# Twelve weight transfers issued from inside the first attention, and two attentions that normalise their own input

## The reference

```python
# layer 0, attention (retention-like decay on the probabilities)
q, k, v = split(layernorm(x) @ W_attn)         # 128 -> 3 x 128, 16 heads of 8
probs   = softmax(q k^T / sqrt(8), masked) * decay
x       = x + (probs v) @ W_proj

# layer 1, attention (no projections: the normed input itself is scaled)
xn    = layernorm(x)                            # eps 1e-5, no gain
q, k  = xn * rotation, xn * entangle
x     = x + softmax(q k^T / sqrt(8)) xn
```

## Time and profile before

| | |
|---|---|
| median of three executions | 1744.04 us |
| the profiled execution's own time | 1747.32 us |
| its span in the trace | 1745.5 us |
| mean granted TensorE clock | 0.922 |
| TensorE matmul busy | 1506.1 us (86%) |
| VectorE busy | 1171.3 us (67%) |
| ScalarE busy | 902.2 us (52%) |
| GpSimd busy | 716.9 us (41%) |
| layernorm block of the first attention begins | 12.14 us |
| first row maximum of the first attention | 30.34 us |
| layernorm block of layer 1's attention begins | 347.6 us |
| first row maximum of layer 1's attention | 358.17 us |

### The profile page before, as it was taken

How to read it: one execution, slowest core, us unless ns; L and a number is a source line. 1 busy time by engine, 2 the same in 40 slices (tenths; PEclk the granted TensorE clock), 3 DMA queues, 4 the chain that set the end, 5 groups by cost and what they waited for, 6 DMA issues and landing times. The chain is left out here.

```text
span 1745.5 us, 28828 instructions
## 1 busy us (share of the span) xinstructions
PE 1506.1 (86%) x9987; PEld 965.2 (55%) x9987; DVE 1171.3 (67%) x2471; ACT 902.2 (52%) x2612; POOL 716.9 (41%) x674
## 2 busy tenths in 40 slices
PE   4998767879889999978899879999958877679998
PEld 2565535545567765443334337888744343357776
DVE  4887573469777765537998887777767785544443
ACT  2775332257677762226776646777724342444443
POOL 2557251122564441217888882333522234431000
PEclk8999986989999999978999999999979786889999
DMA  6000000000000000020000000000000000000000
GB/s 283 1 2 1 2 2 1 0 1 1 2 2 2 2 1 1 2 87 1 0 1 1 0 1 2 2 2 2 2 0 1 0 1 1 1 1 7 7 6 7
DMA packets 3165, 18.95 MB, mean 11 GB/s; under 512 B 592, under 2 KB 720, under 8 KB 2256
## 3 DMA queue, kind: packets, MB, share of 16 engines
q1 hardware_dynamic: 3024, 17.14, 2.4%
HBM read 16.09 MB, written 1.05 MB: 10 GB/s over the span
## 5 line engine op out<-in xcount | busy, mean ns | idle before, releaser
L827 POOL TENSOR_TENSOR l_xattn_probs<-l_xattn_probs,l_xattn_recip 128x512 f32<-128x512 f32 x128 | 133.3, 1042 | 222.8 <-DVE l_xattn_recip L766 222.4
L999 ACT ACTIVATE l_attn_probs<-ps,l_attn_neg_max 128x128 f32<-128x128 f32 x512 | 145.1, 384 | 74.0 <-DVE l_attn_neg_max L1048 72.2
L2547 POOL TENSOR_TENSOR l_mamba_hc<-l_mamba_h,l_mamba_c 128x512 f32<-128x512 f32 x128 | 159.2, 1272 | 0.0
L2449 DVE TENSOR_TENSOR_SCAN l_mamba_h<-ps,l_mamba_dBx 128x512 f32<-128x512 f32 x128 | 152.6, 1211 | 1.8 <-ACT ps L2346 0.7
L2219 PE MATMUL ps<-l_mamba_hc,w_const 128*128 128x512 f32 x256 | 136.6, 637 | 19.5 <-POOL l_mamba_hc L2547 16.5
L3195 DVE SCALAR_TENSOR_TENSOR xn<-ps,l_gates,xn 128x128 f32<-128x128 f32 x224 | 63.2, 344 | 121.7 <-PE ps L2852 120.8
L761 DVE COPY l_xattn_probsT<-ps 128x512 f32<-128x512 f32 x128 | 87.9, 687 | 71.3 <-PE ps L613 71.3
L2985 ACT ACTIVATE wkv<-ps,w_early 128x512 f32<-128x512 f32 x112 | 70.8, 684 | 115.5 <-PE ps L2841 115.4
L2852 PEld LDWEIGHTS ps<-w_early,wkv 128*128 128x128 f32 x896 | 109.1, 194 | 28.6 <-issue 18.7
L2852 PE MATMUL ps<-w_early,wkv 128*128 128x128 f32 x896 | 111.3, 278 | 8.8 <-ACT wkv L2985 8.8
L712 ACT ACTIVATE l_xattn_probs<-ps,l_xattn_neg_max 128x128 f32<-128x128 f32 x256 | 91.9, 389 | 41.3 <-DVE l_xattn_neg_max L756 41.3
(11 more groups left out here) (523 smaller groups left out, 3666.1 us busy)
## 6 DMA issues: line engine op xcount, KB each, us to landing
w_early<-in_l_moe SPq DMA_DIRECT2D x1, 3669.0 KB, 12.1
w_l_xattn<-in_l_xattn SPq DMA_DIRECT2D x1, 2176.0 KB, 22.6
w_early<-in_l_xattn SPq DMA_DIRECT2D x1, 1890.0 KB, 15.4
w_l_attn<-in_l_attn SPq DMA_DIRECT2D x1, 1242.0 KB, 24.6
ctx<-in_ctx SPq DMA_DIRECT2D x1, 1088.0 KB, 11.1
x<-in_x SPq DMA_DIRECT2D x2, 512.0 KB, 4.4
ctxT<-in_ctxT SPq DMA_DIRECT2D x1, 1024.0 KB, 9.0
out_x<-x SPq DMA_DIRECT2D x4, 256.0 KB, 2.8
```

The costliest lines, as they stand in the source:

```text
L827: nc.gpsimd.tensor_tensor(probs[:, D % 2, n, :, :], probs[:, D % 2, n, :, :], along(recip[:, D % 2, n, :], [P, HALF, P]), ALU.mult).then_i ...
L999: ins = nc.scalar.activation(probs[:, t % 4, g, :], S_of(t)[:, g * P:(g + 1) * P], ACT.Exp, bias=neg_max[:, t % 2, g:g + 1], accum_out=total)
L2449: nc.vector.tensor_tensor_scan(flat(h[:, t % 2, half, :, :]), G.ps[:, DA_BANK[half], :], flat(dBx[:, t % 2, half, :, :]), 0.0, ALU.mult, A ...
L2547: nc.gpsimd.tensor_tensor(heads4(hc[:, t % 4, half, :]), h[:, t % 2, half, :, :], c_sb[:, t % 3, :, :], ALU.mult).then_inc((hc0_set, hc1_s ...
```

## The change

The first block issues four transfers only: blocks 0 to 7 of `x`, the constants, blocks 8 to 15 of `x`, the first attention's weights. The other twelve are issued by SyncE at the start of the attention's own block (`load_rest`). In the first block VectorE takes the statistics of all 16 blocks and the variances of the first eight, and GpSimd their scales. Both narrow attentions lose their layernorm block: they build a `Lead` with banks 4, 5, 6 and 6, and its pieces are woven into their own lists. Quads 0 and 1 are transposed ahead of step 0, quad 2 in step 0 and quad 3 in step 1, each behind the scores. For the first attention GpSimd makes the last scales and normals before the first keys, for layer 1's after them. The small constants move to the start of VectorE's list, the `q_scale` of layer 1 too.

```diff
-def narrow_attention(nc, G, tag, w=None, q_scale=None):
+def narrow_attention(nc, G, tag, w=None, q_scale=None, prepare=None):
...
+        O_BANK, X_BANK = 6, 7
+        lead = Lead(nc, G, s, tag, (4, 5, O_BANK, O_BANK))
...
+        @block.sync
+        def _(sp):
+            if first:
+                load_rest(nc, G, sp)
+            lead.sync(sp)
...
             def project(b):
+                lead.wait(pe, b)
...
+            pe.wait_ge(G.loaded["const"], 16)
+            lead.needs(pe)
+            lead.tensor(pe, 0)
             if projected:
                 project(0)
+                pe.wait_ge(consts, 1)
                 pe.wait_ge(p_taken, 1)
-            else:
-                pe.wait_ge(masked, 2)
+            lead.tensor(pe, 1)
             for t in range(STEPS + OUT_LAG + 1):
                 b, s_ = at(t)
                 if t < STEPS:
                     scores(t)
                 if projected and s_ == 0 and b + 1 < NB:
                     project(b + 1)
+                if t < 2:
+                    lead.tensor(pe, 2 + t)
                 if T_LAG <= t < STEPS + T_LAG:
+                    if t == T_LAG:
+                        lead.wait(pe, QUAD)
                     turn(t - T_LAG)
                 if V_LAG <= t < STEPS + V_LAG:
+                    if t == V_LAG:
+                        lead.wait(pe, NB - 1)
                     times_v(t - V_LAG)
...
+            lead.scalar(act, 0)
             if projected:
                 act.wait_ge(masked, 2)
                 take(0)
+            lead.scalar(act, 1)
             for t in range(STEPS + V_LAG + 1):
...
                 if projected and s_ == 0 and b + 1 < NB:
                     take(b + 1)
+                if t < 2:
+                    lead.scalar(act, 2 + t)
...
+            lead.rest.early(dve, nc.vector, 0, 0)
+            dve.wait_ge(G.loaded["const"], 16)
+            if first:
+                small_constants(nc, G, dve).then_inc(consts, 1)
+            if prepare:
+                lead.needs(dve)
+                prepare(dve)
             heads = G.c["heads"].rearrange("p (r i) -> p i r", r=4)
             nc.vector.tensor_reduce(mask4[:], heads, AX.X, ALU.max).then_inc(masked, 1)
             nc.vector.memset(v_sb[:, :, :, DH:VP], 0.0).then_inc(masked, 1)
...
+            lead.rest.variances(dve)
+            for q in range(1, lead.rest.first // QUAD):
+                lead.rest.early(dve, nc.vector, 0, q)
+            lead.rest.late(dve, nc.vector, 0)
             for t in range(STEPS + OUT_LAG + 1):
...
+            lead.rest.early(pool, nc.gpsimd, 1)
             pool.wait_ge(masked, 2 if projected else 3)
-            keys(0)
+            if projected:
+                lead.rest.scales(pool)
+                lead.rest.late(pool, nc.gpsimd, 1)
+                keys(0)
+            else:
+                keys(0)
+                lead.rest.scales(pool)
+                lead.rest.late(pool, nc.gpsimd, 1)
...
 def l0_attn(nc, G):
-    layernorm(nc, G, "l0_attn", "l0_attn")
     narrow_attention(nc, G, "l0_attn", w=G.w["l0_attn"])
...
-        layernorm(nc, G, "l1_attn", "l1_attn", also=prepare)
-        narrow_attention(nc, G, "l1_attn", q_scale=q_scale[:])
+            dve.wait_ge(own, 1)
+
+        narrow_attention(nc, G, "l1_attn", q_scale=q_scale[:], prepare=prepare)
...
+    @G.first.vector
+    def _(dve):
+        for b in range(NB):
+            if b % (NB // 2) == 0:
+                dve.wait_ge(G.loaded[f"x{b // (NB // 2)}"], 16)
+            if b == begun.first:
+                begun.variances(dve)
+            begun.stats(b)
+        dve.wait_ge(begun.seen, NB)
+
+    @G.first.gpsimd
+    def _(pool):
+        nc.gpsimd.memset(G.neg_half[:], -0.5).then_inc(exponent, 1)
+        pool.wait_ge(exponent, 1)
+        begun.scales(pool)
+
+
+def load_rest(nc, G, sp):
+
+    for group in LAYOUT:
+        if group == "l0_mlstm":
+            sp.dma_start(G.ctxT[:], G.aps["ctxT"]).then_inc(G.loaded["ctxT"], 16)
+            sp.dma_start(G.ctx1, G.aps["ctx1"]).then_inc(G.loaded["ctx1"], 16)
+        if group not in ("const", "l0_attn", "l3_moe"):
+            sp.dma_start(G.pack[group], G.aps[group]).then_inc(G.loaded[group], 16)
```

More of the change, by code:

```diff
@@ L851, in narrow_attention @@
     OUT_LAG = V_LAG + (2 if projected else 1)
+    first, G.started = not G.started, True
     with Scope(nc, G, tag) as s:
@@ L866, in narrow_attention @@
         (masked, p_made, p_taken, q_set, v_set, k_ready, scored, maxed, exped, row_summed, row_inverted, evened, turned, copied, summed,
-         o_copied, o_turned, inverted, normed, out_made, added) = (s.sem(n) for n in (
+         o_copied, o_turned, inverted, normed, out_made, added, consts) = (s.sem(n) for n in (
              "masked", "p_made", "p_taken", "q_set", "v_set", "k_ready", "scored", "maxed", "exped", "row_summed", "row_inverted",
-             "evened", "turned", "copied", "summed", "o_copied", "o_turned", "inverted", "normed", "out_made", "added"))
+             "evened", "turned", "copied", "summed", "o_copied", "o_turned", "inverted", "normed", "out_made", "added",
+             "consts"))
+        O_BANK, X_BANK = 6, 7
+        lead = Lead(nc, G, s, tag, (4, 5, O_BANK, O_BANK))
         ahead = Ahead(nc, G, s, twice=not projected)
         DONE = OUT_LAG + U * ahead.first
-        O_BANK, X_BANK = 6, 7
         Q, K, V, E = (slice(n * P, (n + 1) * P) for n in range(4))
@@ L1074, in keys @@
                 else:
+                    lead.wait(pool, b)
                     source = G.xnT[:, b, :]
@@ L3388, in _, with load @@
             received_normals(LAST)
-def load(nc, G, aps):
+def load(nc, G, aps, with_stats):
+    s = Scope(nc, G, "load")
+    begun = Ahead(nc, G, s, first=NB // 2) if with_stats else None
+    exponent = s.sem("exponent")
     @G.first.sync
@@ L3401, in _ @@
               .then_inc(G.loaded[f"x{n}"], 16)
-        for group in LAYOUT:
-            if group == "l3_moe":
-                continue
+            group = ("const", "l0_attn")[n]
             sp.dma_start(G.pack[group], aps[group]).then_inc(G.loaded[group], 16)
-            if group == "l0_attn":
-                sp.dma_start(G.ctxT[:], aps["ctxT"]).then_inc(G.loaded["ctxT"], 16)
-                sp.dma_start(G.ctx1, aps["ctx1"]).then_inc(G.loaded["ctx1"], 16)
+    if not with_stats:
+        return
+    @G.first.vector
[19 more added lines that the diff above has]
+            sp.dma_start(G.pack[group], G.aps[group]).then_inc(G.loaded[group], 16)
 def small_constants(nc, G, dve):
@@ L3416, in small_constants @@
     nc.vector.tensor_copy(G.rows3_bf[:], G.c["rows3"])
-    nc.vector.tensor_copy(G.mask_qk_bf[:], G.c["mask_qk"])
     nc.vector.tensor_copy(G.mask_kq_bf[:], G.c["mask_kq"])
+    return nc.vector.tensor_copy(G.mask_qk_bf[:], G.c["mask_qk"])
 def store(nc, G, out):
@@ L3487, in program @@
             G.first = first
-            load(nc, G, aps)
+            load(nc, G, aps, (sublayers or SUBLAYERS)[0] is l0_attn)
         for sublayer in sublayers or SUBLAYERS:
```

## The result

The changed kernel takes 1735.89 us in the median (1721.68 to 1740.54, 20 executions), the kernel before 1744.53 (1734.31 to 1755.77, 20). The medians differ by 8.6 us, or 0.5%. The ratio of the means is 0.9934 (11.5 us), 95% interval 0.991 to 0.9959: faster, clear of noise and by under 1%. The forecast was 1735.1 us. The profiled execution has a span of 1736.6 us against 1745.5, 8.9 less, which is the very sum that was forecast. That it fits to the decimal is luck: two of the parts came out better than forecast, one worse, and that is what the rest of this is about.

A forecast was written before the change was run, and what follows sets the result against it. Serial links from each narrow attention's start to its first row maximum were taken as the bound. 6.0 us in the first attention plus 2.9 in layer 1 gave 8.9, from 1744.04 to 1735.1 us; the forecast's own range 1727 to 1743.

The forecast's parts named there:

- The first block: Start: second half of `x` lands at 8.0 us, the attention's block opens at 11.1 instead of 12.18.
- Rival (d): Start: moved issues don't free it, as `x`'s second half lands late; at 12 us, 4 us go: 1739; chance 0.05.
- The first preamble: First attention up to its first row maximum: keys done at 20.15, row maximum at 23.3, 7.0 us earlier.
- Given back in steps 0 and 1: First attention: transposes of quads 2 and 3 between the scores cost 1.0 us, between 0.5 and 2.0, leaving 6.0 gained.
- rival (b): First attention and layer 1: TensorE's clock stays up, both ramps save 2 to 3 us more each; 1730; chance 0.08.
- Layer 1: Layer 1's attention: first row maximum 4.4 us earlier, 1.5 us given back before the third scores, 2.9 us gained.
- rival (c): TensorE's clock stays at half into the full steps because it waits twice; four such steps lose 15 us: 1750; chance 0.07.
- The port: VectorE and GpSimd normals: exclusion would delay first keys by up to 1.6 us, first attention giving 4.4; left out of the sum.
- The stages between take the time they took: Stages between first attention and layer 1's attention: sign that their time stays unchanged, 0 us gained.
- everything later follows at its own pace: Opening claim: only the stretches up to each attention's first row maximum matter; what follows keeps its pace.
- The sum: Whole kernel: 6.0 from the first attention plus 2.9 from layer 1, 8.9 us gained.

The follow-up runs named there:

- the mLSTM experiment: The kernel before plus one wait keeping GpSimd's last two pairs of query quads until VectorE's five row operations are done; 1742.78 us, ratio 0.9958.

## Why the prediction was right, point by point

- **The first block** held. `x` landed at 4.79 and 7.85 us (said: 4.5 and 8.0), the block opened at 11.04 (11.1), and the late issue was worth 1.07 us by the experiment that took it back (1.1). Rival (d) is out.
- **The first preamble** held: keys done at 20.17 (20.15), first row maximum at 23.32 (23.3). The sum of row durations carried the whole serial chain to 0.1 us.
- **Given back in steps 0 and 1** failed. I took 1.0 us; the piece gained 8.0 and not 6.0. 7.0 of the 8.0 lie ahead of the first row maximum, as forecast, so from there to the stage's end the new form took 0.95 us less, not 1.0 more. The second row maximum came 4.86 us after the first, before 3.49, but only a part of that is quad 2: where the old code's second scores ran at half pace too, in the mLSTM experiment, it was 4.45. And the third scores took 1.13 us after and 2.02 before, and the ramp was faster from there. That looks like rival (b), for this stage alone; I had priced it at 2 to 3 us and given it 0.08. It is not the change's own doing as far as the runs show. From first row maximum to end the old code took 141.95, 141.95 and 140.93 us in three kernels, the new code 140.6 to 142.2 in the seven without idle matmuls there besides the changed kernel's 141.00. The two ranges overlap: neither a loss of 1.0 us nor a gain can be told from how the clock happened to run, and the 1.0 us was a term too much.
- **Layer 1** held in its mechanics: first row maximum 5.95 us behind the boundary at 337.18 (said 6.2 behind 347.6), third scores 5.05 us later (5.1). The 2.9 us are 3.3 at like clock. In the profile of the changed kernel the stage is nevertheless 2.2 us longer than before, since it met a clock of 0.87 instead of 0.93. That is 5.1 us between forecast and profile, a third of the 15 us of rival (c), but not by rival (c)'s reason, the two waits of the new ramp: the same ramp behind the old start kept 0.93, and the old form behind the new start had 0.86. The step that failed is again that the stage would meet the conditions that it met before.
- **The port** was misjudged. I set the rule aside because normals side by side took 1.0 us together. That was true of normals, and is after: six take 1.83 us beside GpSimd's two at 1.68, where alone they would be about 1.6. GpSimd's two early normals did take 2.16 us, beside VectorE's normals, memset and casts. And side by side is not cheap for all operations. In layer 1's new preamble one operation on four columns took 0.89 us beside GpSimd's keys and 0.17 elsewhere, and in the mLSTM the scan and the subtraction waited for whole GpSimd operations. The Trainium skill ("SBUF — State Buffer", Who interferes with whom) says that the shared port pair is held for a whole instruction by whichever of the two engines starts first, VectorE taking part in a two-port mode or with two SBUF inputs. The mLSTM rows agree: 2.06, 1.80 and 1.72 us against 0.42, 0.29 and 0.23 alone, GpSimd's at 1.9. The late normals here don't go by turns: 1.83 us is far from the 3.3 that turns would give.
- **"The stages between take the time they took"** was wrong: 2.5 us less. The step that failed is the opening claim that everything later follows at its own pace. A shift of half a microsecond in how VectorE and GpSimd meet was enough, and the price of the meeting, up to 3.1 us by the experiment, stood in no term of the sum.
- **The sum** of 8.9 is thus 8.0 + 2.5 - 2.2 + 0.6 in the profile. The 20 executions on each side give 8.6 by the medians and 11.5 by the means, so the forecast is right in size, in the profile by terms that cancel: 2.0, 2.5 and 0.6 us too little against 5.1 too much. What of the total is mechanics and what is clock can't be split: the rest of the program alone varies by 10 us.

## What to carry to other kernels

A boundary or a layernorm block that is taken away pays what its serial links cost, and such a chain can be summed from single rows to 0.3 us or better here. What comes behind it can't: look for operations of VectorE and GpSimd that run side by side on SBUF, and for places where TensorE's clock falls and comes back, because a shift rearranges both. Before you name the cause of a slow clock, run the old code behind the new start and the new code behind the old one: here that took the blame from the code. When the expected gain is 0.5%, compare pieces of the timeline at like clock before you believe a total.

## What the runs showed of the hardware that was not expected

- A VectorE scan of 128x128 took 2.06 us and a subtraction 1.80 us beside GpSimd products of 128x1024 (1.93 each), and 0.42 and 0.29 us without them. One wait on GpSimd gained 3.1 us in the piece.
- Idle matmuls in layer 1's ramp, five and three, went with a clock of 0.87 instead of 0.70 over 40 us and 4.8 us gained in one kernel, and with 116.4 us instead of 118.7, 2.3 us, in another. Five in the first attention's ramp brought its first scores from 2.08 to 1.13 us and the third from full to half pace, 2.6 us lost.
- The same work of TensorE at the same distances from a boundary met two courses of the clock: full pace again 19.7 us behind it in one kernel, 24.8 in the other.
- Early in the program the granted clock read 1.00 while four scores took 2.08 us; at a granted 1.00 later they took 1.13.
- Twelve transfers in flight (DMA share 0.85 to 0.92 in the first attention's ramp) did not slow GpSimd's keys: those of 128x512 took 1.03 us under them and 1.04 us later.
